# A decoder layer on one core: constant products ahead of TensorE's waits, and the last pairs of heads weighed in fp32

## The reference, cut to what matters

```python
def _L0_attn_ref(x, Wq, bq, Wk, bk, Wv, bv):
    ...
    scores = jnp.einsum('bgkqd,bkld->bgkql', q, k) * SCALE
    causal = jnp.tril(jnp.ones((T, T), dtype=bool))
    scores = jnp.where(causal, scores, jnp.float32(-jnp.inf))
    w = jax.nn.softmax(scores, axis=-1)
    out = jnp.einsum('bgkql,bkld->bgkqd', w, v)
    ...
x = x + _L0_attn_ref(_layernorm(x, axis=-1), Wq, bq, Wk, bk, Wv, bv)
x = x + _L0_xattn_ref(_layernorm(x, axis=-1), ctx_1024, ctx_1024, 0, mask_SxS2_ff0)
x = x + _L0_ffn_ref(_layernorm(x, axis=-1), gate_q, gate_absmax, up_q, up_absmax, down_q, down_absmax)
```

## Time and profile before

| | us |
|---|---|
| median of 3 runs | 2607.57 (2604.19 to 2608.82) |
| the profiled execution | 2597.22 |
| its span in the profile | 2595.4 |
| PE busy in it | 2448.5 (94%) |
| DVE, ACT, POOL busy | 1768.3, 1646.6, 1526.2 |

### The profile page before, as it was taken

The page is one execution under the profiler, slowest core; times in us unless marked ns, Lnnn a source line. Parts: engine busy times, 40 slices in busy tenths (PEclk is TensorE's granted clock), DMA queues, the critical chain, the costliest instruction groups (busy, mean ns, idle before and its releaser), DMA issues.

```text
span 2595.4 us, 48461 instructions
## 1 busy us (share of the span) xinstructions
PE 2448.5 (94%) x17800; PEld 1347.4 (52%) x17800; DVE 1768.3 (68%) x2984; ACT 1646.6 (63%) x3006; POOL 1526.2 (59%) x1367
## 2 busy tenths in 40 slices
PE   7999999999985568999999999999999999999999
PEld 4667777777664454444444444444444444444444
DVE  6656777767777866777777777777777897645311
ACT  4566666666666557777777777877777786545100
POOL 2556677777769576777777777777776343212100
PEclk9999999999997679999999999999999999999999
DMA  6353443333332311222222222222323844333231
GB/s 219 90 161 94 121 129 118 111 115 101 91 95 85 98 57 45 91 92 90 90 82 82 90 86 86 93 87 91 93 78 106 276 130 147 107 91 109 69 111 74
DMA packets 224827, 271.09 MB, mean 104 GB/s; under 512 B 36560, under 2 KB 147664, under 8 KB 224592
## 3 DMA queue, kind: packets, MB, share of 16 engines
q1 hardware_dynamic: 224592, 268.00, 32.9%
HBM read 192.94 MB, written 73.40 MB: 103 GB/s over the span
## 4 chain that ended last, share of the span: by engine, by line
PE 53%; POOL 3%; issue 2%; DVE 1%; ACT 1%; DMA 0%; DVEq 0%; ACTq 0%; POOLq 0%
PE ps L2196 31%; PE ps L2229 22%; POOL q_rows L533 1%; POOL p L514 1%; POOL xn L2103 1%; POOL xT L503 0%; DMA h_parts<-xn 0%; DVE p L482 0%; POOL x_row L2109 0%; DVE ps L482 0%; ACT q_rows L529 0%; DVE xT L497 0%; ACT w_l L472 0%; ACT xn L2290 0%; POOL k_rows L533 0%
## 5 line engine op out<-in xcount | busy, mean ns | idle before, releaser
L482 DVE TENSOR_TENSOR ps<-ps,w_l 128x512 f32<-128x512 f32 x672 | 444.7, 694 | 245.9 <-ACT w_l L472 166.5
L1044 POOL TENSOR_TENSOR arena<-p,arena 128x512 f16<-128x512 f32 x320 | 371.1, 1168 | 218.2 <-ACT arena L1528 217.5
L503 POOL TENSOR_TENSOR xT<-xT,nat 128x512 f32<-128x512 f32 x162 | 206.6, 1275 | 452.5 <-DVE xT L497 452.5
L472 ACT ACTIVATE w_l<-proj 128x512 f32<-128x512 int32 x672 | 400.9, 622 | 67.8 <-DVE ps L482 52.1
L1520 ACT ACTIVATE p<-ps 128x512 f32<-128x512 f32 x320 | 191.2, 597 | 256.5 <-PE ps L1296 251.5
L1741 DVE TENSOR_REDUCE block_max<-ps 128x4 f32<-128x512 f32 x320 | 219.1, 688 | 167.8 <-PE ps L1267 165.2
L469 ACT ACTIVATE ps<-proj,small 128x512 f32<-128x512 int32 x336 | 218.1, 682 | 166.0 <-DVE xT L497 164.8
L2196 PE MATMUL ps<-arena,q_rows 128*128 128x512 f16 x1344 | 296.4, 380 | 5.4 <-DVE x_row L2378 3.8
L2458 DVE SCALAR_TENSOR_TENSOR arena<-ps,arena 128x1024 f32<-128x1024 f32 x70 | 85.2, 1221 | 211.4 <-PE ps L2229 208.5
L1237 PE MATMUL ps<-xT,w_h 128*128 128x512 f16 x720 | 217.9, 385 | 1.5 <-DVE xT L1695 1.5
L2196 PEld LDWEIGHTS ps<-arena,q_rows 128*128 128x128 f16 x1344 | 131.6, 98 | 165.9 <-issue 7.6
(11 more groups left out here) (255 smaller groups left out, 5929.6 us busy)
## 6 DMA issues: line engine op xcount, KB each, us to landing
proj<-in_codes SPq DMA_DIRECT2D x168, 256.0 KB, 2.9
nat<-in_scales SPq DMA_DIRECT2D x336, 128.0 KB, 2.9
h_parts<-xn SPq DMA_DIRECT2D x112, 256.0 KB, 2.3
nat_parts<-nat SPq DMA_DIRECT2D x48, 256.0 KB, 2.0
q_rows<-nat_parts SPq DMA_DIRECT2D x96, 128.0 KB, 2.7
w_l<-h_parts SPq DMA_DIRECT2D x21, 448.0 KB, 4.1
x_unit<-in_x SPq DMA_DIRECT2D x64, 128.0 KB, 2.7
x<-x_unit SPq DMA_DIRECT2D x64, 128.0 KB, 2.3
```

Source lines behind the costliest of these rows:

```text
L472: op = self.nc.scalar.activation(out, self.t.codes[:, t % 2, :], ACT.Copy, scale=slope, bias=intercept)
L482: self.nc.vector.tensor_tensor(other if n == self.LUT - 2 else held, held, other, ALU.max).then_inc(self.lut, 1)
L503: self.nc.gpsimd.tensor_tensor(self.quarter(t), self.quarter(t), self.t.scales[:, t % 2, :], ALU.mult)\
L1044: nc.gpsimd.tensor_tensor(p_l[:, n % 2, k, :], p32[:, f % 3, :], p_h[:, n % 2, k, :], ALU.subtract).then_inc(p_low, 1)
```

## The change

**Bursts.** A new function `stay_busy` issues eight bf16 products of 128x128 from constants (the identity and the causal mask) into bank 3 or bank 1 of PSUM, whose contents nobody reads at that time; it waits until the turnings that last used the bank have been read. It is called from step 59 on: in odd steps before the chunks 1 to 4, in even steps before chunk 0 (24 calls, of which 14 in the steps 59 to 63). In `last_cross` it is called behind each score, each turn and each weighing up to round 15 (45 calls).

**Fp32 weighing.** The pairs 56 to 63 (from `WIDE` on; the last two units) are weighed by `weigh_wide`: twenty fp32 products of 128x33 instead of sixty fp16 ones. Their 40 chunks have no `high_part` on ACT and no `low_part` on POOL. `exps` writes them into a ring of 13 buffers, the three of `p32` and ten cut from the memory of the fp16 halves, and waits for weighings instead of for POOL. `weigh_wide` waits for the five exponentials of its pair. The values of the units 14 and 15 stay fp32 in `v32`; the instruction on DVE that made their low halves becomes a memset of the column of ones.

**Memory.** `v_parts` shares its memory with `v32`, and the moments of the feed forward move into the arena, which grows by 16 words; at the start POOL has one memset more. SP's list is the same.

```diff
-        self.v_parts = carve([P, 2, QT, PAIRS, 2 * D + 1], FP16)
+        values = carve([P, 2, QT * PAIRS * (D + 1)], FP32)
+        self.v32 = values.rearrange("p b (q j n) -> p b q j n", q=QT, j=PAIRS)
+        self.v_parts = [values[:, b, 0:QT * PAIRS * (2 * D + 1) // 2].bitcast(FP16)
+                        .rearrange("p (q j n) -> p q j n", q=QT, j=PAIRS) for b in range(2)]
...
-        self.vx_last = arena[:, 13336:13336 + KVX * 2 * (D + 1)].rearrange("p (g n) -> p g n", g=KVX)
-        self.px_last = self.v_parts[:].rearrange("p b q j n -> p (b q j n)")[:, 0:4 * HALF].bitcast(FP32) \
-            .rearrange("p (b n) -> p b n", b=2)
+        self.vx_last = arena[:, 13352:13352 + KVX * 2 * (D + 1)].rearrange("p (g n) -> p g n", g=KVX)
+        self.px_last = values.rearrange("p b n -> p (b n)")[:, 0:2 * HALF].rearrange("p (b n) -> p b n", b=2)
...
+        self.p_wide = [buf[:].rearrange("p b k n -> p (b k n)").bitcast(FP32)[:, HALF * k:HALF * k + HALF]
+                       for buf in (self.p_h, self.p_l) for k in range(CHUNKS)]
...
+    BUSY_FROM = NS - 5
+    WIDE = NS - 2 * PAIRS
+    RING = 3 + 2 * CHUNKS
...
+    def wide_p(f):
+        n = (f - CHUNKS * WIDE) % RING
+        return p32[:, (CHUNKS * WIDE + n) % 3, :] if n < 3 else t.p_wide[n - 3]
...
             for f in (5 * s - 4, 5 * s - 3):
-                if 0 <= f < CHUNKS * NS:
+                if 0 <= f < CHUNKS * WIDE:
                     low_part(f)
...
                 shift(x, s32[:, x % 2, :])
             for f in (5 * s - 2, 5 * s - 1):
-                if 0 <= f < CHUNKS * NS:
+                if 0 <= f < CHUNKS * WIDE:
                     low_part(f)
...
-            if 0 <= 5 * s < CHUNKS * NS:
+            if 0 <= 5 * s < CHUNKS * WIDE:
                 low_part(5 * s)
...
+        def weigh_wide(n):
+            u, j = n // PAIRS, n % PAIRS
+            if j == 0:
+                pe.wait_ge(v_low, u + 1)
+            pe.wait_ge(t_exp, CHUNKS * (n + 1))
+            pe.wait_ge(max_out, min(n // 2 + (n % 2), NS // 2 - 1) + 1)
+            pe.wait_ge(o_read, n)
+            for qt in range(QT):
+                for hh in range(2):
+                    col = (D + 1) * (2 * qt + hh)
+                    for kt in range(qt + 1):
+                        k, at = t_place(hh, kt, qt)
+                        mm = nc.tensor.matmul(bank[O_BANK][:, col:col + D + 1], wide_p(CHUNKS * n + k)[:, at:at + P],
+                                              t.v32[:, u % 2, kt, j, :], start=(kt == 0), stop=(kt == qt))
+            mm.then_inc(o_done, 1)
...
             for k in range(CHUNKS):
+                if s >= BUSY_FROM and (k > 0 if s % 2 else k == 0):
+                    stay_busy(PROJ_BANK + 1)
                 if 0 <= s + 2 < NS:
...
                     x_weigh(y, XO_BANK, px_h, px_l)
                 if k == 4 and 1 <= s <= NS:
-                    weigh(s - 1)
+                    (weigh if s - 1 < WIDE else weigh_wide)(s - 1)
                 if kind_in(s) is not None and k < 4 and s != -2:
                     project(kind_in(s), k)
+
+        def stay_busy(dst):
+            if dst == PROJ_BANK + 1:
+                pe.wait_ge(ln_low, turned_in[dst])
+                pe.wait_ge(*kind_read(NP * B - 1))
+                if pairs_turned[0]:
+                    pe.wait_ge(feed.x_summed, 5 * pairs_turned[0])
+            else:
+                pe.wait_ge(ln_low, 2 * len(LN_ORDER))
+            for n in range(8):
+                nc.tensor.matmul(bank[dst][:, 0:P], t.ident_b[:, :], t.mask_qk[:, :], start=True, stop=True)
 
         def last_cross():
...
                     x_score(x, LS_BANK, xT[:, rt, :, :, :])
+                    stay_busy(PROJ_BANK + 1 if n < 10 else LN_BANK)
...
                     x_turn(x - 2, LT_BANK, p32[:, (x - 2) % 3, :])
+                    stay_busy(PROJ_BANK + 1 if n < 10 else LN_BANK)
                 if n >= 3:
...
                     last_weigh(x - 3)
+                    if n < NX:
+                        stay_busy(PROJ_BANK + 1 if n < 10 else LN_BANK)
...
-            nc.scalar.activation(t.v_parts[:, u % 2, :, :, 0:D],
+            values = t.v_parts[u % 2] if PAIRS * u < WIDE else t.v32[:, u % 2, :, :, :]
+            nc.scalar.activation(values[:, :, :, 0:D],
                                  proj32[:, 1, :].rearrange("p (q j d) -> p q j d", q=QT, d=D), ACT.Copy)\
...
-            if f >= 3:
+            n = f - CHUNKS * WIDE
+            if 3 <= f and n < 3:
                 act.wait_ge(p_low, f - 2)
-            nc.scalar.activation(p32[:, f % 3, :], bank[T_BANK + T_OF[f % CHUNKS]][:, :], ACT.Exp,
+            elif n in (3, 3 + CHUNKS):
+                act.wait_ge(o_done, WIDE)
+            elif n >= RING:
+                act.wait_ge(o_done, WIDE + (n - RING) // CHUNKS + 1)
+            nc.scalar.activation(p32[:, f % 3, :] if n < 0 else wide_p(f), bank[T_BANK + T_OF[f % CHUNKS]][:, :], ACT.Exp,
                                  scale=SELF_SCALE).then_inc(t_exp, 1)
...
                     v_part(v_cut_in(s))
-                if k != 3 and 0 <= f - 1 < CHUNKS * NS:
+                if k != 3 and 0 <= f - 1 < CHUNKS * WIDE:
                     high_part(f - 1)
-                if k == 2 and 0 <= f < CHUNKS * NS:
+                if k == 2 and 0 <= f < CHUNKS * WIDE:
                     high_part(f)
...
 
         def v_low_part(u):
             dve.wait_ge(v_high, u + 1)
-            nc.vector.tensor_tensor(t.v_parts[:, u % 2, :, :, D + 1:2 * D + 1],
+            if PAIRS * u >= WIDE:
+                nc.vector.memset(t.v32[:, u % 2, :, :, D:D + 1], 1.0).then_inc(v_low, 1)
+                return
+            nc.vector.tensor_tensor(t.v_parts[u % 2][:, :, :, D + 1:2 * D + 1],
                                     proj32[:, 1, :].rearrange("p (q j d) -> p q j d", q=QT, d=D),
-                                    t.v_parts[:, u % 2, :, :, 0:D], ALU.subtract).then_inc(v_low, 1)
```

More of the change, by code:

```diff
@@ L74, in sb @@
             return ctx.enter_context(nc.sbuf_tensor(name, shape, dt))
-        arena = sb("arena", [P, 14360], FP32)
+        arena = sb("arena", [P, 14376], FP32)
         self.taken = 0
@@ L101, in __init__ @@
         self.bias_v = carve([P, KV * D], FP32)
-        self.vx_last = arena[:, 13336:13336 + KVX * 2 * (D + 1)].rearrange("p (g n) -> p g n", g=KVX)
-        self.px_last = self.v_parts[:].rearrange("p b q j n -> p (b q j n)")[:, 0:4 * HALF].bitcast(FP32) \
-            .rearrange("p (b n) -> p b n", b=2)
+        self.vx_last = arena[:, 13352:13352 + KVX * 2 * (D + 1)].rearrange("p (g n) -> p g n", g=KVX)
+        self.px_last = values.rearrange("p b n -> p (b n)")[:, 0:2 * HALF].rearrange("p (b n) -> p b n", b=2)
         self.f_stats = arena[:, 14336:14360].rearrange("p (w h n) -> p w h n", w=2, h=2)
+        self.f_moments = arena[:, 14360:14376].rearrange("p (b w n) -> p b w n", b=2, w=2)
         self.w_h = sb("w_h", [P, CT, 4 * HALF], FP16)
@@ L232, in __init__ @@
         self.stats = t.f_stats
-        moments = sb("f_moments", [P, 2, 2, 4], FP32)
+        moments = t.f_moments
         self.mean_var, self.var_eps, self.rstd = moments[:, :, :, 0:2], moments[:, :, :, 2], moments[:, :, :, 3]
@@ L1120, in _ @@
         pool.wait_ge(ln_xn, 4)
-        cleared = [t.ident_b, t.mask_qk, t.mask_kq, t.v_parts, t.kx_h, t.kx_l, t.vx_h, t.vx_l]
+        cleared = [t.ident_b, t.mask_qk, t.mask_kq, t.v32, t.kx_h, t.kx_l, t.vx_h, t.vx_l]
         for buf in cleared:
@@ L1132, in _ @@
                                 pattern=[[1, P]], channel_multiplier=-1).then_inc(selected, 1)
-        nc.gpsimd.memset(t.v_parts[:, :, :, :, D:D + 1], 1.0).then_inc(selected, 1)
-        pool.wait_ge(selected, 5)
+        for b in range(2):
+            nc.gpsimd.memset(t.v_parts[b][:, :, :, D:D + 1], 1.0).then_inc(selected, 1)
+        pool.wait_ge(selected, 6)
         nc.gpsimd.memset(t.k_rows[96:97, :, :, :], 1.0).then_inc(selected, 1)
         for j in range(2):
-            pool.wait_ge(selected, 6 + j)
+            pool.wait_ge(selected, 7 + j)
             nc.gpsimd.memset(t.vx_h[TC * j:TC * j + TC, :, (D + 1) * j + D:(D + 1) * j + D + 1], 1.0)\
                 .then_inc(selected, 1)
-        pool.wait_ge(selected, 8)
+        pool.wait_ge(selected, 9)
         for s in range(0, TO):
@@ L1314, in weigh @@
                         low = p_l[:, n % 2, k, at:at + P]
-                        v = t.v_parts[:, u % 2, kt, j, :]
+                        v = t.v_parts[u % 2][:, kt, j, :]
                         out = bank[O_BANK]
@@ L1444, in _ @@
             if s == -2:
-                pe.wait_ge(selected, 8)
+                pe.wait_ge(selected, 9)
             step(s)
@@ L1606, in _ @@
             if s == -2:
-                act.wait_ge(selected, 8)
+                act.wait_ge(selected, 9)
             step(s)
@@ L1734, in v_low_part @@
             dve.wait_ge(v_high, u + 1)
-            nc.vector.tensor_tensor(t.v_parts[:, u % 2, :, :, D + 1:2 * D + 1],
+            if PAIRS * u >= WIDE:
```

(7 more changed lines are left out.)

## The result

The changed kernel is slower: 2630.33 us in the median of 7 runs (2619.03 to 2639.07) against 2605.46 before (2601.23 to 2609.0); the ratio is 1.0093, with an interval from 1.0078 to 1.0108. That is 24 us, where 11 fewer were forecast. It is the side of the third rival (2624).

The account below looks back on a forecast made before the run. POOL was taken to bound 780 to 825 us, PE the parts before and behind the stretch where other engines set the time. The terms 3 - 9 - 2 - 3 = -11 us took 2607.57 to 2597 us, range 2581 to 2617.

Parts of the forecast that it names:

- the third rival: Slower, chance 0.19: PE at the low clock becomes the bound, 742 to 825 us takes 95 instead of 83; 2624 us.
- I take the full clock, as in 700 to 742, where PE had hardly a gap either.: 742 to 825 us: PE's work is priced at full clock, 70 us; at mean clock 0.77 it would be 91.
- The weighing's price: Fp32 weighing of each of eight pairs: 4.5 us at full clock, 3.0 us more than the fp16 products.
- the argument that the moving columns don't set the pitch: Fp32 weighing: transposes of 128 columns keep practically the pitch of products of 66, so 0.111 us per record was taken.
- The bound for pair 56: End of step 57, before 742 us: bounds -0.5 and, with the clock at 1.00, little above +3 us.
- the +3: Pair 56, weighed at the end of step 57 where PE has no idle time: +3.0 us.
- The relief: 742 to 825 us: POOL loses 32 low halves, 38.1 us, and ACT 32 high halves, 17 us by estimate.
- the -9: 742 to 825 us, steps 58 to 63: 74 us for 83, bounds -17 to +12.
- the -2: 825 to 868 us: POOL's arrears, ACT's high halves and quicker pair turns, less pair 63's weighing: -2 us (-5 to +4).
- the rival of the larger gain: Chance 0.12: PE is hidden, DVE's 66 us bound 742 to 825 us; -27 in sum, 2581 us.
- The bursts: 0.48 us each: 14 in steps 59 to 63, about 7 us; 45 in 868 to 965 us, stretch forecast -3.
- The second rival: No difference, chance 0.22: waits alternate, the clock is not held; 742 to 825 us takes 78, bursts +1; 2607 us.

Follow-up runs that it names:

- relief alone: Kernel before, last eight pairs weighed with twenty fp16 products of the high halves alone, low halves left out, no bursts: 2594.56 us, ratio 0.9951.
- fp32 only: Changed kernel without bursts, last eight pairs weighed in fp32 with 33 moving columns: 2629.43 us, ratio 1.0078 to the kernel before.

## Why the prediction was wrong

**The step that failed: "I take the full clock, as in 700 to 742, where PE had hardly a gap either."** With it, PE's work from 742 us was put at 70 us, and the stage at 74; PE was busy for 86.20 us at a clock of 0.79, in a stage of 95.70. The fp32 weighing itself takes the clock down, without a gap before it in pair 56, and leaves it down for what follows; and where the clock is down ahead of a weighing, as behind a wait ahead of pairs 61 and 63, the weighing does not bring it back. By the two kernels without bursts that differ in the columns alone this is 0.78% - 0.00%, 20 us: nearly all of the 24. By the two with bursts it is 0.93% - 0.22%, some 18 us.

**The weighing's price** at full clock was right (4.6 us, 4.5 forecast), and so was the argument that the moving columns don't set the pitch: 33 and 132 columns keep 0.11. That the columns might matter for the clock was not seen. The bound for pair 56, "since the clock is 1.00 there, little above +3", broke for this reason: from the maxima of pair 58 to those of pair 60 the changed kernel takes 27.7 us for 23.3, 4.4 lost on the first weighing. With 132 columns, where the clock stays at 1.00 in pair 56, it takes 26.4, so the +3 was right for the full clock. The eight weighings with 132 columns and no bursts cost 13 us against relief alone (1.0000 - 0.9951), of the 41.1 - 5.6 = 35.5 by which their records are longer than there; for the rest there was room in PE's waits (in relief alone PE is busy for 47.43 of 74.8 us).

**The relief** was in the forecast, as part of the -9 and the -2, and it is there: up to 13 us, with PE's shorter weighings in it. With PE's price taken out, DVE is nearest to the bound (64.57 of 74.8 us), as the rival of the larger gain had it, but the stage becomes 4.6 us shorter and not 17.

**The bursts** were priced at their 0.48 us (0.45 to 0.47 measured from start to next start) and at a gain of about 3 us in the last cross attention. The mean clock rose there, the gain is not there: with bursts of 8 the transposes behind the wait stayed at the low clock, and three bursts stand between the two halves of a turn, on the very path that was to become shorter. For that stretch the forecast set the bursts against PE's idle time only. They cost 0.12% (0.03 to 0.20).

**The third rival** had the place and the sign. That its 95 us for the stage met the 95.7 measured is luck in part: it had 12 us more on a stretch of 83, and 16.3 more on one of 79.4 were measured. Its mechanism was half right. PE at the low clock is the bound, and ahead of the weighings of pairs 61 and 63, the two of 8.7 us, the clock does fall about a wait of PE for DVE (2.22 and 2.49 us). But the first fall came in step 57, in the middle of a weighing, and with 132 columns the same waits cost far less, since the clock comes back within the weighing. The second rival had the bursts about right (+1 forecast, +3 measured) and the weighing wrong.

The Trainium skill, "TensorE: Matmul & The Clock Gate", section "What's actually happening", has the clock follow how busy TensorE was of late. By busy time as the profile counts it the trace disagrees: PE was busy without a pause to 754.4 us when the clock fell, and 8.69 us of uninterrupted records did not raise it. The measurement decides: with the same loads, and PE busy throughout, the weighing of pair 56 lost the full clock with 33 columns and kept it with 132.

The sum with the measured terms: relief -13, weighing with 132 columns +13, the clock +20, bursts +3, places 0, makes +23 for a measured +24. The first three are differences along one row of kernels, from before to fp32 only, and add up to its 0.78% by their making; only the term of the bursts tests the sum.

What stays open: why some weighings with 33 columns ran at the full clock to their end, or nearly, and others not. With bursts it was those of the odd steps, which have four bursts ahead of them (pairs 58, 60 and 62); without any burst pairs 57, 58 and 60 took 4.6 us too, and 61 to 63 took 8.7. In the changed kernel pairs 56 to 60 and 62 began at 1.00, and 61 and 63 at 0.50; why it fell inside 56, 57 and 59, and in 58 just before its end, and not inside 60 and 62, no run here shows. Column counts between 33 and 132 were not run either.

## What to carry to other kernels

Before three fp16 products are replaced by one in fp32, count records and loads, and look how many columns each moves: the same 40 loads with 33 columns cost this kernel 20 us more than with 132, by what the clock does to everything behind them. Here the products could be widened from 33 to 132 columns for some 0.1 us per weighing (4.6 to 4.7). And constant products that are to raise a clock have a price of their own: look what stands behind each of them, and whether they come between two pieces of work for which others wait.

## What the hardware showed that was not expected

- Fp32 products with 33 moving columns took the granted clock from its upper level to the lower in the middle of a weighing (751.3 to 757.2 us), with no idle time before them; in five weighings, 40 records in a row at the low clock (8.7 us) did not bring it back. With 132 columns the pitch was the same 0.11 us, and all eight weighings that began at the low clock came back to the full one before their end.
- Bursts of 24 constant products raised the clock from 0.67 to 1.00 over 97 us, and the kernel became 0.26% slower: between two halves of a turn they cost 4.02 us and gave back 1.6.
